# Routing passes of a mixture-of-experts layer spread over five attention batches

## What is computed

```python
xn = _layernorm(x)
Wdkv = xn @ latent_w + latent_b                       # [b, t, 36]
q = einsum('btc,hcl->bhtl', xn, Wd_w) + Wd_b
scores = where(causal, einsum('bhtl,bsl->bhts', q, Wdkv) / sqrt(8), -inf)
z = softmax(scores) @ Wdkv                            # per head, then @ out_w + out_b
probs = softmax(xn @ Wr + br)                         # 8 experts
gate, idx = max(probs), argmax(probs)
y = onehot(idx) . (relu(xn @ W1[e] + b1[e]) @ W2[e] + b2[e]) * gate
x = x + z @ out_w + out_b + y
```

## Time and profile before

| | us |
|---|---|
| median of 3 runs | 1682.36 (1680.28 to 1682.92) |
| profiled execution, its own time | 1689.08 |
| its span, first to last instruction | 1687.3 |
| TensorE busy | 1470.3 (87% of the span) |
| VectorE / ScalarE / GpSimd busy | 1149.8 / 993.0 / 931.1 |
| mean granted TensorE clock | 0.94 of full |

### The profile page before, as it was taken

How to read it: one execution, slowest core, us unless ns; L and a number is a source line. 1 busy time by engine, 2 the same in 40 slices (tenths; PEclk the granted TensorE clock), 3 DMA queues, 4 the chain that set the end, 5 groups by cost and what they waited for, 6 DMA issues and landing times.

```text
span 1687.3 us, 44051 instructions
## 1 busy us (share of the span) xinstructions
PE 1470.3 (87%) x12833; PEld 1046.1 (62%) x12835; DVE 1149.8 (68%) x4098; ACT 993.0 (59%) x2496; POOL 931.1 (55%) x1659
## 2 busy tenths in 40 slices
PE   4989999999999999989993888888888888867873
PEld 4535555555555555559993777777777777756762
DVE  5666666666666666635552898998998998966650
ACT  5445555555555555543333888888888888842331
POOL 6456666666544444434445666666666666613663
PEclk9789999999999999999996999999999999985775
DMA  9032222222222222343330212112112211226434
GB/s 228 1 73 63 66 64 65 64 64 64 59 54 65 66 66 65 77 92 82 69 68 18 45 43 43 44 44 43 44 44 42 45 44 42 45 42 122 89 80 117
DMA packets 240984, 107.60 MB, mean 64 GB/s; under 512 B 145561, under 2 KB 229338, under 8 KB 240858
## 3 DMA queue, kind: packets, MB, share of 16 engines
q1 hardware_dynamic: 228074, 89.56, 22.6%
q0 software_dynamic: 10240, 13.64, 3.7%
q10 hardware_dynamic: 2608, 3.67, 0.8%
HBM read 61.92 MB, written 40.16 MB: 60 GB/s over the span
## 4 chain that ended last, share of the span: by engine, by line
PE 63%; ACT 16%; issue 5%; DVE 5%; POOL 4%; DMA 4%; SPq 1%; POOLq 0%; another core or an unknown queue 0%; ACTq 0%; DVEq 0%
PE bankA L1806 8%; PE bankT L1829 8%; PE bankB L1854 7%; PE bankT L2008 4%; PE bankB L1870 3%; PE bankT L1838 3%; PE bankB L1861 3%; ACT qx L1596 3%; ACT km L1605 2%; ACT gqx L1596 2%; PE bankT L2127 2%; PE bankA L2109 2%; ACT rows L1669 2%; PE bankT L2132 2%; PE bankT L1997 2%
## 5 line engine op out<-in xcount | busy, mean ns | idle before, releaser
L966 DVE CUSTOM_DVE_ANT_0 masked<-bankS,causal 128x128 bf16<-128x128 f32 x512 | 128.8, 288 | 231.5 <-PE bankS L1819 227.5
L664 POOL TENSOR_SCALAR_AFFINE_SELECT probs<-probs 128x512 f32<-128x512 f32 x256 | 171.6, 695 | 125.8 <-ACT probs L1509 124.8
L1509 ACT ACTIVATE probs<-bankT 128x1024 f32<-128x1024 f32 x128 | 131.3, 1026 | 116.0 <-PE bankT L1829 116.0
L969 DVE CUSTOM_DVE_ANT_0 masked<-bankS,causal 128x256 bf16<-128x256 f32 x512 | 195.5, 419 | 0.1
L657 POOL CAST qb<-qT 128x256 bf16<-128x256 f32 x256 | 100.1, 415 | 130.2 <-ACT qT L1504 130.2
L1504 ACT ACTIVATE qT<-bankA,bd 128x256 f32<-128x256 f32 x256 | 107.5, 471 | 92.1 <-PE bankA L1806 88.1
L1806 PE MATMUL bankA<-xnT,wd 128*128 128x256 f32 x512 | 149.4, 415 | 0.0
L1829 PE MATMUL bankT<-qT,kT 37*128 37x512 f32 x512 | 147.1, 651 | 0.7 <-ACT probs L1509 0.7
L1854 PE MATMUL bankB<-probs,vaug 128*64 128x512 f32 x512 | 139.9, 625 | 6.2 <-POOL probs L664 2.0
L1317 DVE STREAM_TRANSPOSE pt<-pe 128x768 f32<-128x768 f32 x128 | 124.4, 972 | 25.6 <-ACT pe L1582 25.6
L1517 ACT COPY yT<-bankB 128x512 f32<-128x512 f32 x128 | 75.0, 586 | 108.4 <-PE bankB L1861 108.4
(11 more groups left out here) (304 smaller groups left out, 4140.2 us busy)
## 6 DMA issues: line engine op xcount, KB each, us to landing
rzb<-reciprocals SPq DMA_DIRECT2D x128, 128.0 KB
yT<-yT SPq DMA_DIRECT2D x64, 128.0 KB
xtab<-tab SPq DMA_DIRECT2D x32, 192.0 KB, 2.0
xs_sorted<-zeros SPq DMA_DIRECT2D x1, 4608.0 KB, 18.2
qT<-xs_sorted SPq DMA_DIRECT2D x144, 32.0 KB, 1.8
ys_sorted<-qT SPq DMA_DIRECT2D x36, 128.0 KB, 1.9
value_rows<-vrow SPq DMA_DIRECT2D x32, 128.0 KB, 1.8
vx<-value_rows SPq DMA_DIRECT2D x256, 16.0 KB, 1.9
```

The lines of the kernel that those rows point to most:

```text
L664: pool.affine_select(out=blocks, in_=blocks, compare_op=ALU.is_ge, fill=0.0, base=0, pattern=[[0, 4], [1, P]], channel_multiplier=-1).then ...
L966: dve.tensor_tensor_reduce(masked[:, e, 0:P], bankS[:, e, 0:P], causal[:, P:2 * P], -1.0, -NEG, ALU.add, ALU.min, mneg[:, n.half, e, j, 0:1])
L969: ins = dve.tensor_tensor_reduce(masked[:, e, P:3 * P], bankS[:, e, P:3 * P], causal[:, :], -1.0, -NEG, ALU.add, ALU.min, mneg[:, n.half, ...
L1509: act.activation(pT[:, g % 2].rearrange("p e j t -> p e (j t)"), bankT[:, 0:2, :], ACT.Exp, scale=SCALE0).then_inc(S["exp_done"], 1)
```

## The change

The routing passes go over the steps of three batches (with the one-hots before and `gates0` and `owners` behind them, five) and not two. On TensorE the first score product and a projection go ahead of `rank(0)`, and `rank(1)` goes behind `st_second`. On GpSimd one quarter of the masks is built in each of four steps, behind the second clip. The scatter starts two batches later, with its wait, so that `CLEARED` is 10; the expert weights follow three a pair, and the last of them lies inside the loop.

```diff
-        CLEARED = 1 + NT // SCATTER // 2
+        ROUTED = 2
+        CLEARED = ROUTED + NT // SCATTER // 2
...
-                experts(2 * (i - CLEARED))
+                experts(3 * (i - CLEARED))
                 maxima(Batch(i + 1, 1))
                 denominators(Batch(i + 1, 0))
-                experts(2 * (i - CLEARED) + 1)
-            for k in range(2 * (LOOP - CLEARED), E0 + KF + 1):
-                experts(k)
+                for k in range(3 * (i - CLEARED) + 1, min(3 * (i - CLEARED) + 3, E0 + KF + 1)):
+                    experts(k)
...
-                if groups:
-                    pool.wait_ge(S["qb_sb"], n.b * PAIRS + 4)
-                for g in groups:
-                    layer1_masks(g)
...
                 clip(b, 1)
+                if group is not None:
+                    pool.wait_ge(S["clipped"], b.b * (2 * GROUPS) + 4)
+                    layer1_masks(group)
...
-            step(first, second, Batch(1, 0), None, (0, 1))
-            step(second, Batch(1, 0), Batch(1, 1), None, (2, 3))
+            step(first, second, Batch(1, 0), None, 0)
+            step(second, Batch(1, 0), Batch(1, 1), None, 1)
+            step(Batch(1, 0), Batch(1, 1), Batch(2, 0), None, 2)
+            step(Batch(1, 1), Batch(2, 0), Batch(2, 1), None, 3)
             pool.wait_ge(S["xs_zero"], 16)
             pool.wait_ge(S["te_done"], 1)
-            for pair in range(1, CLEARED):
+            for pair in range(ROUTED, CLEARED):
                 for b in (Batch(pair, 0), Batch(pair, 1)):
-                    step(b, b.next(), b.next().next(), (b.b - 2) * SCATTER)
+                    step(b, b.next(), b.next().next(), (b.b - 2 * ROUTED) * SCATTER)
```

And TensorE's step:

```diff
+                if n:
+                    smax(n, 0)
+                    qproj(n, 1)
                 if ranks:
                     rank(0, onesb)
-                if n:
-                    smax(n, 0)
-                if ranks:
-                    rank(1, strict)
-                if n:
-                    qproj(n, 1)
...
                 st_second(b, 0, prior)
+                if ranks:
+                    rank(1, strict)
```

More of the change, by code:

```diff
@@ L665, in clip, with step @@
                                        pattern=[[0, 4], [1, P]], channel_multiplier=-1).then_inc(S["clipped"], 1)
-            def step(b, n, m, rows=None, groups=()):
+            def step(b, n, m, rows=None, group=None):
                 if n:
@@ L1147, in _ @@
             kv(Batch(1, 0))
+            red(Batch(1, 0), 0)
             totals()
-            red(Batch(1, 0), 0)
+            red(Batch(1, 0), 1)
+            red(Batch(1, 0), 2)
             ranks()
-            red(Batch(1, 0), 1)
+            red(Batch(1, 0), 3)
             invert(first)
-            red(Batch(1, 0), 2)
+            red(Batch(1, 0), 4)
             counts()
[L1155 to L1158, removed]
             red(Batch(1, 0), 5)
+            normalise(first, 0)
@@ L1160, in _ @@
             red(Batch(1, 0), 6)
-            places(1)
-            places(2)
+            normalise(first, 1)
             red(Batch(1, 0), 7)
             turn_maxima(Batch(1, 0), True)
-            for k in range(QUADS // 2 + 1):
-                normalise(first, k)
+            normalise(first, 2)
             kv(Batch(1, 1))
+            red(Batch(1, 1), 0)
+            red(Batch(1, 1), 1)
+            resid(first)
+            red(Batch(1, 1), 2)
+            invert(second)
+            red(Batch(1, 1), 3)
@@ new lines, in _ @@
+            bases()
+            red(Batch(1, 1), 4)
+            places(0)
+            red(Batch(1, 1), 5)
+            places(1)
+            normalise(second, 0)
+            red(Batch(1, 1), 6)
+            normalise(second, 1)
+            red(Batch(1, 1), 7)
+            turn_maxima(Batch(1, 1), True)
+            normalise(second, 2)
+            kv(Batch(2, 0))
+            red(Batch(2, 0), 0)
+            red(Batch(2, 0), 1)
+            resid(second)
+            red(Batch(2, 0), 2)
@@ L1168, in _ @@
+            invert(Batch(1, 0))
+            red(Batch(2, 0), 3)
+            places(2)
+            red(Batch(2, 0), 4)
             places(3)
+            red(Batch(2, 0), 5)
             places(4)
-            step(Batch(1, 1), second, first)
-            kv(Batch(2, 0))
+            normalise(Batch(1, 0), 0)
+            red(Batch(2, 0), 6)
+            normalise(Batch(1, 0), 1)
+            red(Batch(2, 0), 7)
+            turn_maxima(Batch(2, 0), True)
+            normalise(Batch(1, 0), 2)
@@ L1172, in _ @@
+            kv(Batch(2, 1))
             gates0()
-            step(Batch(2, 0), Batch(1, 0), second)
-            kv(Batch(2, 1))
+            step(Batch(2, 1), Batch(1, 1), Batch(1, 0))
+            kv(Batch(3, 0))
             owners()
-            for b in (Batch(2, 0), Batch(2, 1)):
-                step(b.next(), b.before(), b.two_before())
-                kv(b.next().next())
+            step(Batch(3, 0), Batch(2, 0), Batch(1, 1))
+            kv(Batch(3, 1))
             with dve.Fori(3, LOOP) as i:
```

## The result

| | us |
|---|---|
| changed kernel, median of 20 runs | 1688.34 (1682.45 to 1691.69) |
| kernel before, median of 20 runs beside it | 1684.43 (1679.95 to 1688.41) |
| ratio of the two | 1.0019, 95% interval 1.0010 to 1.0028 |
| profiled execution of the changed kernel | 1687.9, span 1686.2 |

The forecast was 1682.2 us, so a change of -0.2 us; measured is +3.9 us by the medians and +3.2 us (1.7 to 4.7) by the ratio, with an interval that excludes no change by a little; 1688.3 lies above the range's end of 1686.6. The base was off as well: the three runs of before that the forecast stood on had a median of 1682.36, all 20 runs beside the changed kernel 1684.43, 2.1 us more. Moved up by these 2.1 us the range would have ended at 1688.7, so that the number fell outside it by the base as much as by the kernel.

What follows compares the result with a forecast made beforehand. The prediction took TensorE, busy 87% of the span, as the bound, with gains only where it stops or runs at half clock. Start +2.8 us and end -3.0 us, together -0.2 on 1682.36, gave 1682.2 us; range 1671.8 to 1686.6.

Runs made afterwards that it cites:

- the run with one pair less: Kernel before with expert weights three a pair, last load inside the loop, starting one pair later, so SP has one pair fewer written out: 1684.43 us, ratio 0.9996.
- the run with the experts' schedule: Kernel before with only the expert weights' schedule changed: three a pair, the last inside the loop, routing unchanged: 1681.0 us, ratio 0.9980.

## What to carry to other kernels

Ask of each loop on the path, also those that a diff doesn't touch, whether it runs at the pace of its busiest engine; if it does not, look for a ring through the issuing engine, in which any small thing counts once a pass. In such a queue put nothing that waits ahead of something that is ready: here storing one pair later was worth 9 to 11 us, and 23 small loads moved behind four urgent transfers 8 to 10 us, each more than the whole rearrangement of passes changed. And when two kernels differ where their code is the same, compare the lengths of their programs: a few idle instructions tell whether a loop's place matters.

## What was not expected of the hardware

- A loop of SP takes 0.24 us more a pass at one place of its program (beginning at instruction 333) than at 341, 349 or 365, with the same instructions: 0.13 us more across the branch, 0.11 more for four transfers.
- GpSimd shows something like it, once. In the changed kernel's program, behind the tile loop, a gather starts after 1.15 us and not after 0.81, with nothing that it waits for; its traces all have it, those with the other engines' code of before have not. Before, then after:

```profile
898.02 0.97 POOL L770 DMA_INDIRECT yg<-ys_sorted,idx_g  x1 [0.81 <-POOL gate_g L766]
```
```profile
901.26 0.97 POOL L771 DMA_INDIRECT yg<-ys_sorted,idx_g  x1 [1.15 <-issue]
```

These 0.34 us reach the start of the second layer (22.20 against 21.86 us). That the place is the cause here too is only argued.
- The same stop doesn't always cost the same clock. The stop of 2.04 us in the routing batch lost 5.1 us in the kernel before and in the run with one pair less, but 1.7 us in the run with the experts' schedule, whose TensorE code is the same; there the clock was at half already in the last microsecond of the stop and back at 102. A stop of 1.09 us on a maximum near 720 us, harmless in six other traces, was once followed by 10 us at half rate.
